# Where the routed experts' factors are applied: to the tokens, or to each unit's silu

## The reference

```python
g = einsum('bsd,edf->ebsf', h, Wg)
u = einsum('bsd,edf->ebsf', h, Wu)
expert_outs = einsum('ebsf,efd->ebsd', silu(g) * u, Wd)
expert_output = einsum('be,ebsd->bsd', gating_probs, expert_outs)
shared = einsum('bsf,fd->bsd', silu(h @ Sg) * (h @ Su), Sd)
out = x + (1.0 - sg) * expert_output + sg * shared       # h = x, sg = shared gate of the batch
```

## Time and profile before

| | us |
|---|---|
| median of 3 runs | 156.97 (156.9 to 157.15) |
| the profiled execution | 156.72 |
| its span | 155.4 |
| instructions | 2306 |

### The profile page before, as it was taken

One profiled execution on the slowest core, in us unless ns is written; L12 is line 12 of the kernel. 1 busy time (PEld: TensorE's weight loads), 2 busy tenths in 40 slices (PEclk: granted clock), 3 DMA queues, 4 the chain that ended last, 5 costly groups with the idle time before them and its releaser, 6 DMA issues.

```text
span 155.4 us, 2306 instructions
## 1 busy us (share of the span) xinstructions
PE 152.1 (98%) x673; PEld 123.9 (80%) x673; DVE 98.4 (63%) x160; ACT 108.9 (70%) x204; POOL 77.3 (50%) x78
## 2 busy tenths in 40 slices
PE   7999999999999999999999999999999999999993
PEld 2688888888888888888888888888888888888873
DVE  0597678765666666666666666666665666666692
ACT  4787876777687757775788577766777687755541
POOL 1578993547255645546354825572547255650000
DMA  4975015005100330015000600050000000000006
GB/s 146 210 201 195 0 35 168 4 2 164 40 0 0 106 103 0 0 34 169 0 0 0 202 0 0 0 202 0 0 0 0 0 0 0 0 0 4 0 0 135
DMA packets 12726, 8.24 MB, mean 53 GB/s; under 512 B 5040, under 2 KB 10672, under 8 KB 12720
## 3 DMA queue, kind: packets, MB, share of 16 engines
q1 hardware_dynamic: 12144, 7.64, 17.3%
q10 hardware_dynamic: 576, 0.52, 1.1%
HBM read 7.64 MB, written 0.52 MB: 53 GB/s over the span
## 4 chain that ended last, share of the span: by engine, by line
PE 94%; DMA 3%; SPq 1%; ACT 0%; issue 0%
PE y_ps L521 10%; PE y_ps L528 10%; PE y_ps L519 10%; PE u_ps L640 9%; PE g_ps L635 9%; PE g_ps L636 9%; PE u_ps L641 9%; PE u_ps L639 9%; PE g_ps L634 9%; DMA w_raw<-in_L_cond_Su 3%; PE g_ps L586 1%; PE g_ps L588 1%; PE u_ps L600 1%; PE u_ps L599 1%; PE u_ps L602 1%; PE g_ps L591 1%
## 5 line engine op out<-in xcount | busy, mean ns | idle before, releaser
L431 DVE TENSOR_TENSOR h_ps<-silu,u_ps 128x512 f32<-128x512 f32 x71 | 49.2, 696 | 48.5 <-PE u_ps L641 44.7
L345 ACT ACTIVATE h_hi<-h_ps 128x512 fp32r<-128x512 f32 x71 | 42.5, 599 | 37.9 <-DVE h_ps L431 37.9
L251 POOL TENSOR_TENSOR w_lo<-w_raw,w_hi 128x384 fp32r<-128x384 f32 x32 | 32.5, 1016 | 38.3 <-ACT w_hi L335 38.2
L436 DVE TENSOR_TENSOR h_lo<-h_ps,h_hi 128x512 fp32r<-128x512 f32 x71 | 48.4, 682 | 0.1
L340 ACT ACTIVATE silu<-g_ps 128x512 f32<-128x512 f32 x72 | 42.8, 597 | 0.0
L256 POOL TENSOR_TENSOR xs_lo<-xs,xs_hi 128x512 fp32r<-128x512 f32 x16 | 20.6, 1290 | 15.8 <-ACT xs_hi L331 15.8
L528 PE MATMUL y_ps<-h_lo,w_hi 128*128 128x512 f32 x71 | 27.6, 389 | 0.0
L521 PE MATMUL y_ps<-h_hi,w_hi 128*128 128x512 f32 x71 | 27.6, 389 | 0.0
L519 PE MATMUL y_ps<-h_hi,w_lo 128*128 128x512 f32 x71 | 27.6, 389 | 0.0
L640 PE MATMUL u_ps<-xs_lo,w_hi 128*128 128x512 f32 x64 | 24.9, 389 | 0.0
L635 PE MATMUL g_ps<-x_lo,w_hi 128*128 128x512 f32 x64 | 24.9, 389 | 0.0
(11 more groups left out here) (81 smaller groups left out, 117.2 us busy)
## 6 DMA issues: line engine op xcount, KB each, us to landing
w_raw<-in_L_cond_Wg SPq DMA_DIRECT2D x8, 256.0 KB, 2.7
w_raw<-in_L_cond_Wu SPq DMA_DIRECT2D x8, 256.0 KB, 3.1
w_raw<-in_L_cond_Wd SPq DMA_DIRECT2D x8, 256.0 KB, 3.5
w_raw<-in_L_cond_Sg ACTq DMA_DIRECT2D x2, 128.0 KB, 3.0
x_nat<-in_x SPq DMA_DIRECT2D x2, 128.0 KB, 2.8
w_raw<-in_L_cond_Sd SPq DMA_DIRECT2D x1, 256.0 KB, 5.0
x_blk<-in_x SPq DMA_DIRECT2D x4, 64.0 KB, 3.4
out<-y_blk SPq DMA_DIRECT2D x4, 64.0 KB, 2.2
```

What stands on the lines that cost most here:

```text
L345: act.activation(h_hi[k % HB][:, :], h_ps[k % BANKS][:, :], ACT.Copy)\
L431: dve.tensor_tensor((to or h_ps[k % BANKS])[:, :], silu[k % BANKS][:, :], u_ps[k % BANKS][:, :], ALU.mult).then_inc(hidden_done, 1)
L436: dve.tensor_tensor(h_lo[k % HB][:, :], h_ps[k % BANKS][:, :], f32(h_hi[k % HB][:, :]), ALU.subtract).then_inc(h_lo_done, 1)
```

## The change

The factor of a routed expert no longer multiplies the tokens. The up matmuls of the routed experts read `x_hi` and `x_lo`, as the gate matmuls do. Instead GpSimd multiplies the silu tile of every routed unit in place by the factors (`scale`), and `hidden` waits for that (`scaled`) instead of for the silu. The factors of an expert are first copied to a small tile of fixed address (`factor`), since the units stand in a loop. `xs`, `xs_hi`, `xs_lo` and what made them are gone, and the waits on them. ScalarE's steps for the next expert are now the four weight slices alone, in units 2, 4, 5 and 6 (`SPLIT_AT`), and GpSimd's `slice_lo` stands behind the scale of the same unit. On VectorE `hidden_lo` of unit n-1 now stands ahead of `hidden` of unit n in the routed experts. The additions to `base_t` stand between expert 7 and expert 8 on GpSimd. In the last unit the scale and `hidden` are done in two halves of 256 columns, and TensorE waits for the second half ahead of `natural(2)`.

```diff
+            def scale(buf, k, n, pieces=1):
+                h = k // NF
+                c = factor[buf][:, h * HBATCH:(h + 1) * HBATCH]
+                pool.wait_ge(silu_done, n + 1)
+                for i in range(pieces):
+                    some = slice(i * NQ // pieces, (i + 1) * NQ // pieces)
+                    t = tokens(silu[k % BANKS][:, :])[:, some, :, :]
+                    by = c.unsqueeze(1).unsqueeze(3).to_broadcast([P, NQ // pieces, HBATCH, PER])
+                    pool.tensor_tensor(t, t, by, ALU.mult).then_inc(scaled, 1)
+
+            def routed(e, buf, nxt=None):
+                pool.tensor_copy(factor[buf][:, :], coef[:, e - 1, :]).then_inc(factor_copied, 1)
+                pool.wait_ge(factor_copied, e)
+                for k in range(UNITS):
+                    last = nxt is None and k == UNITS - 1
+                    scale(buf, k, UNITS * e + k, 2 if last else 1)
+                    if nxt is not None and k in SPLIT_AT:
+                        slice_lo(SPLIT_AT.index(k), *nxt)
...
+            routed(E - 1, 1, (0, NF * (E - 1)))
+
             pool.wait_ge(x_t_done, len(PIECES))
             pool.wait_ge(x1_turned, 1)
             for h in range(HALVES):
                 pool.wait_ge(base_scaled, h + 1)
                 pool.tensor_tensor(base_t[:, h, :], base_t[:, h, :], x_t[:, h, :], ALU.add)\
                     .then_inc(base_done, 1)
+
+            routed(E, 0)
...
-            def split_next(k, buf, halves_before, loads, order=PREPARE):
-                kind, n = order[k - LAG]
-                if kind == "slice":
-                    w_hi_slice(n, buf, loads)
-                else:
-                    xs_hi_half(n, buf, halves_before)
+            def split_next(k, buf, loads):
+                if k in SPLIT_AT:
+                    w_hi_slice(SPLIT_AT.index(k), buf, loads)
...
-            def hidden(n, k, first=False, to=None):
-                dve.wait_ge(silu_done, n + 1)
+            def hidden(n, k, first=False, routed=False):
+                if routed:
+                    dve.wait_ge(scaled, n - UNITS + 1)
+                else:
+                    dve.wait_ge(silu_done, n + 1)
                 dve.wait_ge(up_done, n + 1)
...
             with dve.Fori(2, E) as e:
                 for k in range(UNITS):
-                    hidden(UNITS * e + k, k)
                     hidden_lo(UNITS * e + k - 1, (k - 1) % UNITS)
+                    hidden(UNITS * e + k, k, routed=True)
...
-            hidden(LAST, UNITS - 1, to=h_last)
+            dve.wait_ge(up_done, LAST + 1)
+            for i in range(2):
+                cols = slice(i * HALF_N, (i + 1) * HALF_N)
+
+                dve.wait_ge(scaled, LAST - UNITS + 1 + i)
+                dve.tensor_tensor(h_last[:, cols], silu[(UNITS - 1) % BANKS][:, cols],
+                                  u_ps[(UNITS - 1) % BANKS][:, cols], ALU.mult).then_inc(hidden_done, 1)
...
-                    pe.matmul(u[:, :], hi, xs_hi[buf][:, h, :], start=True, stop=False)
-                    pe.matmul(u[:, :], hi, xs_lo[buf][:, h, :], start=False, stop=False)
-                    pe.matmul(u[:, :], lo, xs_hi[buf][:, h, :], start=False, stop=True)\
+                    pe.matmul(u[:, :], hi, x_hi[:, h, :], start=True, stop=False)
+                    pe.matmul(u[:, :], hi, x_lo[:, h, :], start=False, stop=False)
+                    pe.matmul(u[:, :], lo, x_hi[:, h, :], start=False, stop=True)\
```

More of the change, by code:

```diff
@@ L42, in build @@
     LAST = (E + 1) * UNITS - 1
-    PREPARE = [("slice", 0), ("half", 0)] + [("slice", n) for n in range(1, NF)] + [("half", 1)]
-    FIRST_PREPARE = [("slice", 0), ("slice", 1), ("half", 0), ("slice", 2), ("half", 1), ("slice", 3)]
+    SPLIT_AT = [2, 4, 5, 6]
     assert E % 2 == 0 and NF == 4 and UNITS % HB == 0 and UNITS % BANKS == 0 and NQ == 4
-    assert LAG == BANKS and HB > LAG and UNITS == LAG + len(PREPARE)
+    assert LAG == BANKS and HB > LAG
     ctx = ExitStack()
@@ L80, in build @@
         coef = sbuf("coef", [P, E + 1, B], FP32)
+        factor = [sbuf(f"factor{i}", [P, B], FP32) for i in range(2)]
         ident = sbuf("ident", [P, P], FP32)
@@ L252, in slice_lo @@
                                    f32(w_hi[buf][:, :, n, :]), ALU.subtract).then_inc(w_lo_done, 1)
[L254 to L265, removed]
-                    if kind == "slice":
-                        slice_lo(n, buf, slices_before)
-                    else:
-                        half_lo(n, buf, halves_before)
@@ new lines, in routed @@
+            def routed(e, buf, nxt=None):
[6 more added lines that the diff above has]
+                        slice_lo(SPLIT_AT.index(k), *nxt)
+            for n in range(NF):
+                slice_lo(n, 1, 0)
@@ L273, in gpsimd_program @@
             pool.wait_ge(coef_ready, 1)
+            with pool.Fori(0, E // 2 - 1) as i:
+                for q in range(2):
+                    routed(2 * i + 1 + q, 1 - q, (q, 2 * NF * i + NF * (q + 1)))
+            routed(E - 1, 1, (0, NF * (E - 1)))
             pool.wait_ge(x_t_done, len(PIECES))
             pool.wait_ge(x1_turned, 1)
[L276 to L287, removed]
             for h in range(HALVES):
@@ L430, in hidden @@
                     dve.wait_ge(h_lo_done, n - BANKS + 1)
-                dve.tensor_tensor((to or h_ps[k % BANKS])[:, :], silu[k % BANKS][:, :], u_ps[k % BANKS][:, :],
+                dve.tensor_tensor(h_ps[k % BANKS][:, :], silu[k % BANKS][:, :], u_ps[k % BANKS][:, :],
                                   ALU.mult).then_inc(hidden_done, 1)
@@ L472, in vector_program @@
             for k in range(UNITS):
-                hidden(UNITS + k, k)
                 hidden_lo(UNITS + k - 1, (k - 1) % UNITS)
+                hidden(UNITS + k, k, routed=True)
                 if k == 0:
@@ L480, in vector_program @@
                 for k in range(UNITS):
-                    hidden(UNITS * e + k, k)
                     hidden_lo(UNITS * e + k - 1, (k - 1) % UNITS)
+                    hidden(UNITS * e + k, k, routed=True)
             for k in range(UNITS - 1):
-                hidden(UNITS * E + k, k)
                 hidden_lo(UNITS * E + k - 1, (k - 1) % UNITS)
+                hidden(UNITS * E + k, k, routed=True)
                 if k == NF + 1:
@@ L622, in tensor_program, with routed_expert @@
                 down(k - LAG, k - LAG, 0, begin=(k - LAG) % NF == 0)
-            def routed_expert(base, buf, halves_before, slices_before, first=False):
+            def routed_expert(base, buf, slices_before, first=False):
                 for k in range(UNITS):
@@ L670, in tensor_program @@
             natural(1)
+            pe.wait_ge(hidden_done, LAST + 2)
             natural(2)
```

39 lines of the change are left out of this document (11 added, 28 removed).

## The result

| | before | after |
|---|---|---|
| median, us | 156.9 (156.66 to 157.15, 6 runs) | 224.89 (223.04 to 225.25, 6 runs) |
| ratio | | 1.432 (95%: 1.4287 to 1.4353) |
| profiled execution, its span | 156.72, 155.4 | 224.78, 223.5 |

The account below looks back on a forecast made before the run. TensorE, busy 98%, bounded the kernel before; afterwards a 2.98 us loop through ScalarE's queue would. First routed silu at 21.13, 63 units 187.7, additions 0.8, tail 5.96: span 215.6, forecast 217.2 us; range 213 to 234.

Parts of the forecast that it names:

- The turn on ScalarE's queue: Routed units: the scale joins the loop silu, hidden, h_hi, next silu, which outgrows TensorE's 2.04 us and sets the unit's time.
- The size of the turn: Routed units: 1.85 us a turn, less 0.03, plus 0.08, 1.04 and 0.04, makes 2.98 us.
- The waits with loop counters: GpSimd's and VectorE's waits in looped experts: taken as nothing, with 0.10 us a unit kept as upper end.
- rival B: The scale costs more in its new place, up to 1.29 us: 16 us more, 233 us; chance 6%.
- The cover: Work beside the loop (w_lo, w_hi, h_lo, factor copy, weight loads) costs nothing; w_lo has 0.93 us to spare.
- What was removed: Sixteen each of xs, xs_lo and xs_hi: nothing in the steady stretch, silu(8) at the start 0.29 us earlier.
- The signs: Profile after: silus 2.98 us apart, hidden released by GpSimd, GpSimd busy about 107 us, ScalarE 10 us less, TensorE far under 98%.
- The additions once: Two additions to base_t on GpSimd between experts 7 and 8 delay the scale of unit 64: 0.8 us once.
- The tail: From the last silu to the end, with the last scale in halves: 5.96 us, against 5.75 before.
- Rival A: TensorE's clock falls to the 1.2 GHz level because of gaps in each unit: 240 us; chance 10%.
- Rival C: The scale stays hidden, costing under 0.19 us or with silu(k+1) ahead of h_hi(k): 157 us; chance 2%.

Follow-up runs that it names:

- E2: Changed kernel with ScalarE doing silu(n+1) ahead of h_hi(n) in the routed experts: 158.22 us, ratio to the kernel before 1.009.
- E3: Changed kernel with the scale multiplying only 256 of 512 columns in 63 of 64 units (work left out): 196.99 us.
- E4: Changed kernel with two matmuls instead of three for the routed experts' up product (work left out): 225.2 us.
- E6: Changed kernel without the scale, hidden waiting for the silu (work left out): 156.51 us, ratio to the kernel before 0.9976.
- E1: Changed kernel with VectorE's wait for the scale placed last of the three waits ahead of hidden: 219.8 us.
- E10: Changed kernel with VectorE's wait for the scale in the middle, between those for the up product and h_lo: 218.88 us.
- E7: Changed kernel with six extra 512-column matmuls filling TensorE's idle time ahead of the down product of unit 70: 223.87 us.
- E5: E2 with VectorE taking hidden(n) ahead of h_lo(n-1) in experts 2 to 8, and weight slices at units 2, 4, 6, 7: 173.04 us.
- E9: E5 with one edit, VectorE's wait for the scale placed last: 170.13 us.
- E8: E2 with VectorE taking hidden(n) ahead of h_lo(n-1) in expert 8 alone: 160.22 us.

## Why the prediction was right, and where it was short

- *The turn on ScalarE's queue* (added on the loop): right. E2 opens it and 67 of the 68 us go; E3 shortens the step by 0.43 us and the unit by 0.42 to 0.43; E4 takes work from TensorE and the units stay; E6 takes the step away and all 68 us are back.
- *The size of the turn*: 2.98 forecast, 2.97 measured in experts 1 and 8. The scale is 1040 ns, as xs was the earlier trace rows.
- *The waits with loop counters*: the step that was mis-sized. I took nothing for it, since the earlier trace rows showed 0.10 us once in an expert. It is 0.155 us in each of 48 units, 7.4 us, all of the miss but for the tail, and more than the 0.10 that I kept for the upper end of a unit. The row could not show it: before the change the up product's wait ended last, and in VectorE's queue that wait lies on `hidden` itself in every routed unit but the first of experts 2 to 8, where it lies on a counter step and costs the 0.10 of the row. After the change the wait that ends last is the scale's, and it lies on a counter step in all 48 looped units (E1, E10).
- *The range*: the measured 224.89 is above the 213 to 224 of the forecast itself. It lies in 213 to 234 because that range made more room, up to the 233 of rival B, which did not happen; so the range held by luck at its upper part, not by its working.
- *The cover* of w_lo, w_hi, h_lo and the copy: right. Every scale starts 0.08 us behind its silu, but for the first of expert 7 (0.15) and of expert 8 (0.68, behind the additions).
- *What was removed* gives nothing: right within 0.4% (E6). The 0.29 us at the start can't be told from how much the start varies (20.8 to 21.8 us).
- *The signs*: GpSimd is busy for the 107 us that were foretold. ScalarE is busy for 13 us less instead of 10; its instructions add up to 10.1 us less, and the rest is overlap of their drawn times.
- *The additions once*: 0.6 for 0.8. *The tail*: 5.96 forecast; 5.8 with the clock up (E7), 6.9 as it is.
- *Rival A* (the clock): not in the steady stretch, where the granted clock is 1.00 for 190 us with nine matmuls (2.04 us) in 3.12, but in the tail, for 1.0 us. It was priced as a matter of the units alone. *Rival B*: out, 1040 ns. *Rival C*: its point of decision, ScalarE taking silu(n+1) ahead of h_hi(n), is just what E2 tests, with 158.2 for its 157.

The figure of the Trainium skill (GPSIMD Engine Reference, Performance versus the Vector engine) for GpSimd's two-input operations, by which 512 columns are an estimated 1.11 us, does not fit the broadcast form here: a median of 1.04 over 63 of them. The swinging clock that the Trainium skill describes for frequent short idles (TensorE: Matmul & The Clock Gate, A second HAM failure mode: psum-queue depth-cycling) does not appear with an idle time of some 0.6 us in each unit; here the clock falls behind single longer idle times, in the tail and in expert 8 of E5 and E9.

## What to carry to other kernels

Before you put a step on an idle engine, write down the turn that it joins: follow each in-order queue from one unit to the same place in the next, and add up start to start. An engine at 50% can still be the one that lengthens the turn, and the cure is then the order in the queue (E2: one call moved, 67 us), which gave more than a shorter step (E3: half of the scale, 28 us). And put the wait that will end last where nothing is left to do behind it: in this kernel last in a loop, first in written-out code (no run combines the two). Measure budgets on TensorE from start to start, never from drawn ends.

## What was new on the hardware

- The order of three waits ahead of one VectorE instruction moves its start by 0.03 to 0.21 us behind the event that ends last. The lag is the steps that the queue still has behind that wait: none 0.03, one 0.09 to 0.13, two 0.19 to 0.21 (E1, E10 and the changed kernel). The best place was another one in looped and in written-out code.
- TensorE with 2.04 us of matmuls in 3.12, and idle times of 0.6 us, kept the upper clock for 190 us. An idle time of 1.75 us ahead of the down product of unit 70 was followed by the lower level 0.9 us later; the granted clock was below 1.00 in four of six runs, and in none of six when it was filled. One of 2.35 us (E9) was followed by it after 0.7 us; one of 1.68 us (E8) by none, in five runs.
- A multiplication on GpSimd beside ScalarE's h_hi and VectorE's h_lo (E2) cost them nothing: h_hi 0.599 us, h_lo 0.691, hidden 0.695 and silu 0.598, against 0.600, 0.690, 0.695 and 0.598 without it (E6).
